# Four moves in a one-core kernel of attention, state-space and MoE layers: centroids split early, row numbers written early, first positions signalled apart, and the state stage begun with its first chunk alone

## The reference

```
x = x + 0.5 * ffn(norm(x))      256 -> 1024 -> 256, ternary weights, gelu          norm 0
x = x + attention(norm(x))      16 heads of 16, rotary positions, causal            norm 1
x = x + 0.5 * ffn(norm(x))      the same weights                                    norm 2
x = x + 0.5 * moe(norm(x))                                                          norm 3
x = x + mamba(norm(x))          in_proj, causal conv of 4 taps, silu, scan over     norm 4
                                16 states, gate, out_proj
x = x + 0.5 * moe(norm(x))      the same weights                                    norm 5

moe(x): shared   = swiglu(x, wg_s, wu_s, wd_s) * 0.1
        affinity = sigmoid(x @ centroids.T); top 2 of 16 by affinity + gate_bias
        out      = shared + sum over the two of (affinity / their sum) * expert(x)
```

## Time and profile before

| what | value |
| --- | --- |
| time, median of 3 runs | 938.44 us (932.56 to 939.86) |
| span of the profiled execution | 936.1 us |
| TensorE busy | 713.1 us (76%) |
| VectorE busy | 592.4 us (63%) |
| ScalarE busy | 371.6 us (40%) |
| GpSimd busy | 347.5 us (37%) |
| mean granted TensorE clock | 0.864 |

### The profile page before, as it was taken

One profiled execution on the slowest core, in us unless ns is written; L12 is line 12 of the kernel. 1 busy time (PEld: TensorE's weight loads), 2 busy tenths in 40 slices (PEclk: granted clock), 3 DMA queues, 4 the chain that ended last, 5 costly groups with the idle time before them and its releaser, 6 DMA issues. The chain is left out here.

```text
span 936.1 us, 11120 instructions
## 1 busy us (share of the span) xinstructions
PE 713.1 (76%) x3706; PEld 492.4 (53%) x3706; DVE 592.4 (63%) x1012; ACT 371.6 (40%) x754; POOL 347.5 (37%) x422
## 2 busy tenths in 40 slices
PE   3887887889885987599248578888778879675990
PEld 2766453444333766488146345545445545564880
DVE  6868445767522776344367686788988798662333
ACT  4411334255563322033124844586544444130330
POOL 3223222201112202536310055566656667124462
PEclk9989677779888895899769679999999999867995
DMA  4945622020001910364400000000051000103435
GB/s 179 284 62 94 82 36 37 2 35 2 1 1 55 392 35 13 122 184 165 146 1 0 1 0 1 1 1 1 1 216 54 1 0 1 35 24 129 129 123 174
DMA packets 37640, 65.98 MB, mean 70 GB/s; under 512 B 11618, under 2 KB 27618, under 8 KB 35954
## 3 DMA queue, kind: packets, MB, share of 16 engines
q1 hardware_dynamic: 33074, 52.89, 20.1%
q0 software_dynamic: 4512, 12.39, 3.7%
HBM read 39.65 MB, written 21.69 MB: 66 GB/s over the span
## 5 line engine op out<-in xcount | busy, mean ns | idle before, releaser
L1260 PE MATMUL PS<-FB,C 128*128 128x512 f32 x256 | 134.5, 621 | 4.2 <-DVE FB L1919 3.8
L1360 ACT ACTIVATE FA<-PS 128x512 f32<-128x512 f32 (+3 forms) x192 | 80.7, 496 | 71.5 <-PE PS L1030 71.1
L2045 POOL TENSOR_TENSOR FB<-FB,RBF 128x512 f32<-128x512 f32 x51 | 65.8, 1289 | 81.8 <-DVE FB L1910 81.8
L489 PE MATMUL PS<-C,FB 128*128 128x128 f32 x250 | 45.3, 305 | 57.2 <-DVE FB L1574 30.8
L1996 POOL TENSOR_SCALAR_AFFINE_SELECT FA<-FA 128x128 f32<-128x128 f32 x128 | 36.4, 295 | 129.1 <-ACT FA L1360 126.9
L2026 POOL DMA_INDIRECT GY<-FB x62 | 60.7, 979 | 53.7 <-issue 27.5
L1642 DVE TENSOR_REDUCE FA<-PS 128x2 f32<-128x1024 f32 (+2 forms) x64 | 68.0, 1086 | 19.6 <-PE PS L1009 19.4
L489 PEld LDWEIGHTS PS<-C,FB 128*128 128x128 f32 x250 | 35.6, 158 | 68.5 <-DVE FB L1574 30.9
L1030 PE MATMUL PS<-RA 64*128 64x512 f32 (+3 forms) x192 | 60.2, 496 | 5.4 <-ACT FA L1360 4.9
L1153 PE MATMUL PS<-WE,FB 128*128 x248 | 61.0, 390 | 0.0
L2036 POOL TENSOR_TENSOR FB<-WE,FB 128x512 f32<-128x512 f32 x32 | 42.4, 1325 | 49.3 <-ACT FB L1468 49.3
(11 more groups left out here) (265 smaller groups left out, 1628.1 us busy)
## 6 DMA issues: line engine op xcount, KB each, us to landing
WE<-in_wr SPq DMA_DIRECT2D x8, 1536.0 KB, 11.3
FB<-GX SPq DMA_DIRECT2D x14, 520.0 KB
RA<-RA SPq DMA_DIRECT2D x48, 128.0 KB, 4.8
FB<-GY SPq DMA_DIRECT2D x8, 512.0 KB, 5.7
GX<-GX SPq DMA_DIRECT2D x1, 4030.0 KB, 27.6
GX<-FA SPq DMA_DIRECT2D x1, 3968.0 KB, 16.7
FA<-in_w SPq DMA_DIRECT2D x2, 1024.0 KB, 7.0
FA<-in_qkvo SPq DMA_DIRECT2D x1, 1536.0 KB, 20.6
```

The costliest lines, as they stand in the source:

```text
L489: return pe.matmul(out, in_, ident, start=True, stop=True, is_transpose=True)
L1260: pe.matmul(bank(m), ident, shc[k % 4], start=n == 0, stop=n == DN - 1).then_inc(*yad.inc(ch, n, m))
L1360: act.activation(PT[n % 12][:, c0:], bank(ring_bank[(x, *a)])[:, c0:], ACT.Exp, scale=0.25).then_inc(*exd.inc(*a))
L2045: pool.tensor_tensor(shc[k % 4], sh[k % 5], Cs[(stc.no[ch, n] - 1) % 2], ALU.mult).then_inc(*cma.inc(ch, n, m))
```

## The change

**Centroids.** They get 64 columns of their own memory (CN) instead of a place in a shared area. Their load goes from both `mld` steps to `late`, behind the four weight loads on SyncE and ahead of the GX copy, and is done once. The split becomes a step `cen`, which stands right behind `late` and ahead of norm 2. TensorE's `route` for u = 1 waits for norm 5's planes alone. The memset of `one16` goes to `rank`.

**Row numbers and positions.** A new step `rows`, ahead of `top`, writes the first row numbers on GpSimd once the norm is done. `pos` signals i1 and i2 apart: the eight scatters by i1 wait for the first signal alone, those by i2 and TensorE's second `sgu` for the second.

**State stage.** `An` moves ahead of the `yload`. Norm 4 of chunk 0 stands behind `comb` of tile 3 and takes tiles 4 to 7 between its parts. Norm 4 of chunk 1 moves into `enter_alone`, between chunk 0's projections and convolution taps.

```diff
@@ moe_steps
-    yield [("top", u, 0)]
+    yield [("rows", u), ("top", u, 0)]
@@
-    after = norm_steps(4, 0)
+    if u == 0:
+        yield [("An",)]
     for h in range(NT // 2):
         yield [("yload", u, h)]
-    for t in range(NT):
-        yield [("comb", u, t)]
-        if u == 0 and t >= TC:
-            yield next(after)
-    if u == 0:
-        yield from after
-        yield from norm_steps(4, 1)
+    if u:
+        for t in range(NT):
+            yield [("comb", u, t)]
+        return
+    for t in range(TC):
+        yield [("comb", 0, t)]
+    stat0, stat1, rstd, nrm0, nrm1, tr, xn0, xn1 = norm_steps(4, 0)
+    yield stat0 + stat1 + rstd
+    yield [("comb", 0, TC), ("comb", 0, TC + 1)] + nrm0 + nrm1 + tr
+    yield [("comb", 0, TC + 2)] + xn0 + xn1 + [("comb", 0, TC + 3)]
@@ enter_alone
-    yield proj(0, 0, 1) + conv(0, 0, 0) + proj(0, 2) + conv(0, 0, 1) + proj(0, 3) + conv(0, 0, 2) + proj(0, 4) + conv(0, 0, 3)
-    yield proj(0, 5) + [("silu", 0, 0)] + conv(0, 1, 0) + proj(0, 6) + conv(0, 1, 1, 2) + proj(0, 7) + conv(0, 1, 3)
+    stat0, stat1, rstd, nrm0, nrm1, tr, xn0, xn1 = norm_steps(4, 1)
+    yield proj(0, 0) + stat0 + stat1 + rstd + proj(0, 1) + conv(0, 0, 0) + proj(0, 2) + nrm0 + nrm1
+    yield proj(0, 3) + conv(0, 0, 1) + tr + proj(0, 4) + conv(0, 0, 2, 3)
+    yield proj(0, 5) + [("silu", 0, 0)] + xn0 + xn1 + conv(0, 1, 0) + proj(0, 6) + conv(0, 1, 1, 2) + proj(0, 7) + conv(0, 1, 3)
@@ steps
-    for part in (ffn_steps(0), attention_steps(), [[("late",)]], ffn_steps(1), moe_steps(0), mamba_steps(), moe_steps(1)):
+    for part in (ffn_steps(0), attention_steps(), [[("late",), ("cen",)]], ffn_steps(1), moe_steps(0), mamba_steps(), moe_steps(1)):
@@ sync_program, "late"
                         sp.dma_start(WE[:, i * 3072:i * 3072 + 3072], d["wr"][:, i * 3072:i * 3072 + 3072]).then_inc(*wl[i].inc(0))
+                    sp.dma_start(cenw, d["cen"]).then_inc(*ldm.inc())
                     sp.wait_ge(*gz.at(0, "spare"))
@@ sync_program, "mld"
-                    sp.dma_start(cenw, d["cen"]).then_inc(*ldm.inc(u))
@@ tensor_program, "route"
-                    if ch == 0:
-                        pe.wait_ge(*cen.at(u))
-                        if u == 0:
-                            pe.wait_ge(*xad.at(1, 1))
-                        else:
-                            pe.wait_ge(*mlx.at(TC - 1))
+                    if ch == 0 and u == 0:
+                        pe.wait_ge(*cen.at())
+                        pe.wait_ge(*xad.at(1, 1))
@@ vector_program
-                elif x == "mld":
-                    u, = a
-                    dve.wait_ge(*ldm.at(u))
-                    split(Cn[0].rearrange("p k n -> p (k n)"), Cn[1].rearrange("p k n -> p (k n)"), cenw).then_inc(*cen.inc(u))
-                    dve.memset(one16, 1.0)
+                elif x == "cen":
+                    dve.wait_ge(*ldm.at())
+                    split(CN[:, 0:32], CN[:, 32:64], cenw).then_inc(*cen.inc())
@@ vector_program, "pos"
...
+                    dve.tensor_copy(i1, s1).then_inc(*posd.inc(u, 0))
...
+                    dve.tensor_copy(i2, s2).then_inc(*posd.inc(u, 1))
@@ gpsimd_program
+                elif x == "rows":
+                    u, = a
+                    row = XTs[:, :, D:RW]
+                    pool.wait_ge(*nrm.at(3 + 2 * u, 1, 1))
+                    pool.tensor_copy(row, cst("tok")[:, 0:NT].unsqueeze(2).broadcast_to([P, NT, RW - D])).then_inc(*p_own.inc())
                 elif x == "scat":
                     u, = a
-                    pool.wait_ge(*posd.at(u))
+                    row = XTs[:, :, D:RW]
+                    pool.wait_ge(*p_own.at())
                     pool.wait_ge(*gz.at(1, "copy"))
-                    row = XTs[:, :, D:RW]
-                    pool.tensor_copy(row, cst("tok")[:, 0:NT].unsqueeze(2).broadcast_to([P, NT, RW - D])).then_inc(*p_own.inc())
-                    pool.wait_ge(*p_own.at())
+                    pool.wait_ge(*posd.at(u, 0))
                     for t in range(NT):
                         pool.indirect_dma_start(GX[u], ...)
+                    pool.wait_ge(*posd.at(u, 1))
```

More of the change, by code:

```diff
@@ L455, in build @@
         SM = sb("SM", [P, 320], F)
+        CN = sb("CN", [P, 64], R)
         early = ExitStack()
@@ L561, in build @@
                 ring.append((ring_bank[x], x))
-        ldm = sig("s_ld_cen", of("mld"), 16)
+        ldm = sig("s_ld_cen", [()], 16)
         lds = [sig(f"s_ld_shared{n}", of("mld"), 16) for n in range(2)]
-        cen = sig("s_cen", of("mld"))
+        cen = sig("s_cen", [()])
         rtd = sig("s_route", of("route"))
@@ L576, in build @@
         sad = sig("s_sadd", of("sadd"))
-        posd = sig("s_pos", of("pos"))
+        posd = sig("s_pos", of("pos", 0, 1))
         eidd = sig("s_eid", of("wts"))
@@ L688, in build @@
         ra, fa = Area(RB, NRA2), Area(FB, NFA2)
-        Cn = [ra.take(32).rearrange("p (k n) -> p k n", k=2) for _ in range(2)]
+        Cn = [CN[:, 32 * v:32 * v + 32].rearrange("p (k n) -> p k n", k=2) for v in range(2)]
         WS = [[ra.take(768) for _ in range(2)] for _ in range(2)]
@@ L1697, in vector_program @@
                     u, = a
+                    dve.memset(one16, 1.0)
                     io = cst("iota")[:, 0:16].unsqueeze(1).broadcast_to([P, NT, 16])
@@ L1728, in vector_program @@
                     dve.tensor_tensor(bi, r, base.unsqueeze(1).broadcast_to([P, NT, 16]), ALU.add).then_inc(*d_own.inc())
-                    for o, s_, ii in ((o1, s1, i1), (o2, s2, i2)):
-                        dve.wait_ge(*d_own.at())
-                        dve.tensor_tensor(c3, bi, o, ALU.mult).then_inc(*d_own.inc())
-                        dve.wait_ge(*d_own.at())
-                        dve.reduce_sum(s_, c3, AX).then_inc(*d_own.inc())
-                        dve.wait_ge(*d_own.at())
-                        t = dve.tensor_copy(ii, s_)
-                        if s_ is s1:
-                            t.then_inc(*d_own.inc())
-                    t.then_inc(*posd.inc(u))
+                    dve.wait_ge(*d_own.at())
+                    dve.tensor_tensor(c3, bi, o1, ALU.mult).then_inc(*d_own.inc())
+                    dve.wait_ge(*d_own.at())
+                    dve.reduce_sum(s1, c3, AX).then_inc(*d_own.inc())
+                    dve.wait_ge(*d_own.at())
+                    dve.tensor_copy(i1, s1).then_inc(*posd.inc(u, 0))
+                    dve.tensor_tensor(c3, bi, o2, ALU.mult).then_inc(*d_own.inc())
+                    dve.wait_ge(*d_own.at())
+                    dve.reduce_sum(s2, c3, AX).then_inc(*d_own.inc())
+                    dve.wait_ge(*d_own.at())
+                    dve.tensor_copy(i2, s2).then_inc(*posd.inc(u, 1))
                 elif x == "wts":
```

5 lines of the change are left out of this document (2 added, 3 removed).

## The result

The changed kernel is slower by 1.0%: 945.98 us against 936.15 us (medians of 20 runs each), ratio 1.0098 with a 95% interval of 1.0072 to 1.0123. The profiled execution has a span of 945.5 us at a mean granted TensorE clock of 0.858, against 936.1 us and 0.864 before.

What follows compares the result with a forecast made beforehand. No engine is busy throughout, so waits at four places were taken as the bound. Terms 18.5 - 2.1 - 3.6 - 0.5 - 0.3 - 2.8 + 0.5 = +9.7 us gave 948.1 us on the median; range 940 to 953 us.

Steps and rivals of the forecast that it cites:

- Centroids: End of attention: layer 2's norm waits on VectorE for the centroids, landing behind four loads at 317.6; +18.5 us.
- first rival: Centroid transfer passes the big loads in the queue: stall only 4.8 us, total 934.4 us; chance 10%.
- Both MoE entries: Norm statistics start directly at the residual add's end, without waiting for centroids: -2.1 us first layer, -3.6 us second.
- Scatter: Scatter into expert order starts 1.6 us earlier, but the shared expert's add limits the gain: -0.5 and -0.3 us.
- second rival: Shared expert's add moves with the scatter, so both MoE layers gain 1.6 us: 945.7 us; chance 28%.
- my upper end: Scatter in each MoE layer: the most it could gain, -1.6 us each.
- The first scatter beside VectorE: First scatters run beside VectorE's two-input product; contention would make the fetch's end some 0.2 us worse per layer.
- my tenth or two: Part of the scatter's 1.6 us earlier start given back to memory contention with VectorE: 0.1 or 0.2 us.
- State stage's entry: TensorE projects 8.1 us earlier, second half of the convolution starts earlier: -2.8 us (ends -1, -5).
- third rival: State stage's entry: ScalarE's order and the lower clock take the whole -2.8 and 1 us more: 951.6 us; chance 12%.
- TensorE's clock: State stage's projections: a 3.5 us break lowers the granted clock for 24 matmuls; +0.5 us (0 to +2).

Runs made afterwards that it cites:

- load_third: Changed kernel with the centroid transfer issued after the second of the four 1.5 MB loads instead of after the fourth; one execution, span 936.5 us.
- act_queue: Changed kernel with the centroid transfer issued by ScalarE on its own queue at the same moment; one execution, span 936.0 us.
- split_late: Changed kernel with VectorE's centroid split moved ahead of the first MoE layer's norm, transfer left in place; ratio to the kernel before 0.9906, span 926.0 us.
- cen_only: Kernel before with only the centroid part of the change; ratio to the kernel before 1.0115, span 949.7 us.
- after_again: Changed kernel unchanged, run for a second profile; 645.0 us from the attention's last add to the start of the last add of all.
- before_again: Kernel before unchanged, run for a second profile; 634.4 us from the attention's last add to the start of the last add of all.
- copies_first: split_late with ScalarE's two plane copies put ahead of its two Silus at the state stage's entry; first combine to first scan 74.56 us against 74.55.

## Why the forecast held, point by point

- **Centroids: right.** Landing 317.3 for a forecast of 317.6, stall 18.4 for 18.5, TensorE's first up-projection at 325.92 for 326. It was the sum's largest term by far. load_third and act_queue show one half of it, the order within the queue: half of the loads in front leave 10.9 us of the stall, and another queue leaves 5.2. split_late shows the other half, VectorE's order: with that taken away nothing of the stall is left. The first rival fell. The Trainium skill's rule on completion, cited with the first rival, was not put to the test, since the small transfer never passed the big ones in their queue.
- **Both MoE entries: right**, 2.0 and 3.7 us for 2.1 and 3.6, and again in cen_only without the other parts.
- **Scatter: wrong in size, and in its reason.** I took 0.5 and 0.3 us, because I held the shared expert's add for fixed and nearly last. The profile shows 1.2 and 1.3, near the second rival. Over all profiles, statistics to fetch took 44.3 to 45.6 us with the old scatter (eight values, median 44.8) and 43.4 to 43.9 with the new one (fourteen, median 43.6): 1.2 us. The scatter's start moved by 1.0 us, not by the 1.6 of my upper end, since 0.82 to 0.91 us pass from signal to scatter and not 0.3. The add started 0.04 us behind TensorE, neither the 7.4 of my forecast nor the 5.8 of the second rival. Whether it is late is not decided by the code: in five of twelve executions it came at once in both layers, in seven late in both. When late, it starts 0.1 to 3.6 us behind the end of the last scatter, in all fourteen cases, and never before that end, so a tie to the scatter, as the second rival had it, is not excluded. Where it is late it can be last, as in after_again, and takes back 0.5 us in the first layer and 1.6 in the second; there the 48.50 us from statistics to expert transposes are no less than before (48.28), and the add gates the experts as I had assumed. So the 1.2 us are what the scatter part gives up to the fetch, and the experts get all of it only in the executions in which the add is not last.
- **The first scatter beside VectorE: underrated.** The Trainium skill, "GPSIMD Engine Reference", section 1 (Specifications), had warned of contention while VectorE has two SBUF inputs. It gives no size, and my tenth or two came from no row. These rows fit it: the scatter took 1.6 us with such a product right at its start, 1.1 to 1.25 with later and shorter ones beside it, so it is 0.4 to 0.5. The copy of the row numbers says more, since it is the same instruction in both places. Before, it ran beside this product:

```profile
369.71 0.66 DVE L1743 TENSOR_TENSOR FB<-C,FB 1x496 f32<-1x496 f32 x1
369.74 0.71 POOL L2002 COPY FB<-C 128x32 f32<-128x32 f32 x1 [17.39 <-DVE FB L1735]
```

It took 0.70 or 0.71 us there, in both layers of all four profiles with the copy in its old place, and 0.21 in its new place behind the norm, where VectorE stands idle, in both layers of the other eight: 0.5 us more beside a product of 0.66. The later copy of 128x16 stayed at 0.21 even beside a VectorE operation with one input from SBUF and one from PSUM (before_again, at 848.75). No run took the product away from the scatter alone, so for the scatter the cause is not shown.

- **State stage's entry: right in kind; 1 us too high in this profile, near right over all.** The profile has 1.8 us for 2.8. Over all profiles the second half of the convolution starts 29.3 to 30.4 us behind the first combine with the old entry (four, median 30.0), and 26.5 to 28.0 with the new one (seven without copies_first, median 27.4): 2.6 us. To the first scan it is 76.6 to 77.1 with the old entry, except for cen_only with 74.5, and 74.2 to 74.7 with the new one; the medians differ by 2.2 us, where my -2.8 + 0.5 makes 2.3. That cen_only was as early without the new entry leaves open how much of the gain at the scan is the change's. The spread at the convolution goes with TensorE's clock: in the first 5 us of projections 0.50 or 0.51 was granted in four of the seven, the changed kernel's profile among them, and the first 24 took 8.1 to 8.7 us; in the other three 0.70 to 0.72, and they took 7.1 to 7.2. Either is more than the 24 x 0.253 = 6.1 us that I had taken from 72 projections: that term was too low by 1.1 to 2.6 us. ScalarE's queue, my third rival, was priced too low as well: the wait for the plane copies was 2.0 to 2.3 us, and copies_first shows that 1.0 us of it counts at the convolution and nothing at the first scan. (That rival's sum, the whole 2.8 and 1 us more, is 951.9 and not 951.6.)
- **TensorE's clock: right in sign, at other places.** I expected up to 2 us at one break. The break came (TensorE busy for 2.07 us from 510 to 515, granted clock 0.70 in the next 5 us), but the offset at the first scan is the same +12.64 as ahead of it. The profile has +1.0 in the first scans, +0.7 in the second expert loop and -0.5 in the first. By the repeats these are not shown to be the change's: from the first scan to the second MoE layer's statistics the same stage code took 266.5 to 270.8 us in ten profiles.

The misses (scatter -1.7, state stage +1.0, clock and loops +0.7) cancel to nothing, so the total of +9.35 us for a forecast of +9.7 is closer than its terms deserve: that part is luck. Between the repeats' last adds the difference is 645.0 - 634.4 = 10.6 us. The medians differ by 9.8 us; the level that I forecast, 948.1 us, is 2.1 too high because the median of three runs that I added the shift to was 2.3 above that of twenty.

**Open:** where TensorE's late signal comes from, what makes the first scatter long, and what sets the clock of the projections and of the scans from one execution to the next.

## What to carry to other kernels

Ask of every load that is moved *two* orders: what stands ahead of it in its queue, and what stands behind the first instruction that waits for it on the waiting engine. Here moving the wait away gave 18.4 us back and cost nothing that a trace shows, while the faster transfer on another queue gave 13.2. Taking a wait out of two stages is only a gain if its new place has as much slack as the transfer needs there.

A difference of a few us between two single profiles of this kernel says nothing of the change: the attention's end alone differs by up to 6.6 us and the stage from the first scan on by up to 4.3 us in equal code. It counts only when the place is found at which the offset jumps, and the jump is found again in a second profile. And when two executions are compared for 1 us, compare their granted clock in that stretch first: copies_first looks like no gain against one kernel and like 1 us against another.

## What the runs showed of the hardware

- One queue served four loads of 1.5 MB and a 16 KB transfer one after another, 3.7 us per load, the small one's first packet behind 504 of the loads' 512; the same 16 KB on another queue landed in 4.7 us with the loads in flight, with the packets of both queues in turn (34 and 33 in one microsecond).
- From the end of VectorE's signalling cast to the start of GpSimd's first indirect transfer it took 0.82 to 0.91 us, with GpSimd idle and nothing else to wait for; behind another instruction of GpSimd's own, 0.3 us. A plain copy of GpSimd's started 0.06 to 0.07 us behind such a cast.
- The same GpSimd copy (128x32) took 0.21 us alone and 0.71 us beside a VectorE product of 1x496 with two SBUF inputs.
- In seven of twelve executions VectorE waited 4.7 to 9.7 us for a signal of TensorE's during the scatters, in both MoE layers, where its waits for TensorE were otherwise 1.3 to 4.0; in the other five executions never. Two executions of the same code differ in it.
- The granted clock of the first 30 us of scans lay between 0.79 and 0.92 for the same instructions, and the stage's length went with it, from 270.8 down to 266.5 us.
